# A bidirectional decay scan on VectorE, rewritten as one fp32 matrix product per channel on TensorE

## What is computed

```python
# ek = exp(ctx), v = ctx, ew = exp(w); carries before token t is absorbed
A2 = ew * A + ekt * vt          # and B2 = ew * Bd + ekt, forward and backward in time
cur = jnp.exp(uc + k)
wkv = (Af + Ab + cur * v) / (Bf + Bb + cur)
x = x + tanh(g_xattn) * sigmoid(layernorm(x)) * wkv
# feed-forward, int8 fake quantisation of activations by one maximum over all of them
xq = act_fake_quant(layernorm(x), clip_x)
h = act_fake_quant(silu(xq @ gate.T) * (xq @ up.T), clip_down)
x = x + tanh(g_ffn) * (h @ down.T)
```

## Time and profile before

| | us |
|---|---|
| median of 3 runs | 245.74 (243.35 to 245.87) |
| profiled execution | 245.59 |
| its span | 243.9 |
| attention part, to the first gate product | 153.2 |
| feed-forward part | 90.7 |

### The profile page before, as it was taken

How to read it: one execution, slowest core, us unless ns; L and a number is a source line. 1 busy time by engine, 2 the same in 40 slices (tenths; PEclk the granted TensorE clock), 3 DMA queues, 4 the chain that set the end, 5 groups by cost and what they waited for, 6 DMA issues and landing times.

```text
span 243.9 us, 3531 instructions
## 1 busy us (share of the span) xinstructions
PE 156.2 (64%) x1002; PEld 113.4 (47%) x1002; DVE 219.0 (90%) x307; ACT 166.8 (68%) x220; POOL 121.4 (50%) x151
## 2 busy tenths in 40 slices
PE   0609675476726596556565622999595993689970
PEld 0409565476625485545465612434232341466640
DVE  0999999999999999999999787279999799899993
ACT  5454975929959197393772759799797788689700
POOL 7431444438465384454832740057373575008992
PEclk9955979889999978999987875699998899599995
DMA  5796566610000000000000000000000000002358
GB/s 152 217 336 198 174 203 219 220 50 4 0 0 0 0 0 0 0 0 0 0 0 0 4 0 0 0 1 0 3 0 0 0 0 0 1 3 86 129 180 293
DMA packets 16107, 15.08 MB, mean 62 GB/s; under 512 B 2016, under 2 KB 15840, under 8 KB 16096
## 3 DMA queue, kind: packets, MB, share of 16 engines
q1 hardware_dynamic: 16096, 14.95, 19.2%
HBM read 10.75 MB, written 4.19 MB: 61 GB/s over the span
## 4 chain that ended last, share of the span: by engine, by line
DVE 29%; issue 21%; PE 18%; POOL 14%; ACT 12%; DVEq 2%; DMA 2%; POOLq 1%; SPq 0%; ACTq 0%
DVE hidden L666 9%; PE ps L1012 8%; PE ps L976 7%; DVE hidden L664 3%; POOL rs L357 3%; POOL x_all L334 3%; ACT silu_out L567 2%; POOL hidden L387 2%; POOL hidden L315 2%; DVE h_space L823 2%; DVE h_peaks L789 2%; DMA hidden<-in_ctx 2%; POOL rs L344 2%; DVE hidden L778 2%; DVE x L766 1%
## 5 line engine op out<-in xcount | busy, mean ns | idle before, releaser
L881 PE MATMUL ps<-ident,hidden 128*128 128x128 f32 x128 | 41.4, 323 | 48.5 <-POOL hidden L325 23.7
L881 PEld LDWEIGHTS ps<-ident,hidden 128*128 128x128 f32 x128 | 21.0, 164 | 54.7 <-POOL hidden L325 43.4
L883 PE MATMUL ps<-ident,hidden 128*128 128x128 f32 x128 | 40.2, 314 | 0.0
L885 PE MATMUL ps<-ident,hidden 128*128 128x128 f32 x128 | 40.1, 313 | 0.0
L664 DVE TENSOR_TENSOR_SCAN hidden<-hidden,ps 128x1024 f32<-128x1024 f32 x16 | 36.3, 2269 | 0.0
L666 DVE TENSOR_TENSOR_SCAN hidden<-xq,ps 128x1024 f32<-128x1024 f32 x16 | 36.2, 2262 | 0.0
L443 ACT ACTIVATE hidden<-hidden 128x512 f32<-128x512 f32 x16 | 10.0, 625 | 33.9 <-DVE hidden L677 33.9
L325 POOL TENSOR_TENSOR hidden<-zero_tile 128x18 f32<-128x18 f32 x16 | 3.5, 222 | 56.7 <-DVE hidden L666 56.7
L976 PE MATMUL ps<-xq,wuT 128*128 128x512 bf16 (+1 forms) x96 | 24.8, 402 | 6.4 <-DVE hidden L778 6.2
L1012 PE MATMUL ps<-wdT,z_t 128*128 128x256 bf16 (+1 forms) x192 | 25.4, 288 | 2.6 <-ACT z_t L585 2.6
L789 DVE TENSOR_REDUCE h_peaks<-hidden (+2 forms) x24 | 26.1, 1122 | 0.6 <-POOL hidden L387 0.3
(11 more groups left out here) (91 smaller groups left out, 363.1 us busy)
## 6 DMA issues: line engine op xcount, KB each, us to landing
hidden<-in_ctx SPq DMA_DIRECT2D x8, 512.0 KB, 3.7
x_all<-in_x SPq DMA_DIRECT2D x8, 512.0 KB, 4.6
out<-x_all SPq DMA_DIRECT2D x16, 256.0 KB, 2.2
h_space<-in_L_ffn_w_down SPq DMA_DIRECT2D x1, 704.0 KB, 7.1
z_t<-in_L_ffn_w_gate SPq DMA_DIRECT2D x1, 640.0 KB, 6.2
z_t<-in_L_ffn_w_up SPq DMA_DIRECT2D x1, 640.0 KB, 7.4
z_t<-in_L_ffn_w_gate SPq DMA_DIRECT2D x2, 64.0 KB, 6.4
z_t<-in_L_ffn_w_up SPq DMA_DIRECT2D x2, 64.0 KB, 7.6
```

Source lines behind the costliest of these rows:

```text
L881: nc.tensor.matmul(dst, cur[:, h, q, i * T:(i + 1) * T], ident[:, :], start=True, stop=False, is_transpose=True)
L883: nc.tensor.matmul(dst, scans[:, h, 0, q * UNIT + i * T:q * UNIT + (i + 1) * T], ident[:, :], start=False, stop=False, is_transpose=True)
L885: last = nc.tensor.matmul(dst, scans[:, h, 1, q * UNIT + i * T + 1:q * UNIT + (i + 1) * T + 1], ident[:, :], start=False, stop=True, is_tr ...
```

## The change

The first part is rebuilt. It works on channels, not on groups of sequences:

- `ctx` is loaded whole (8 transfers), and each group is reversed in time by a product with a flipped identity (`reverse`, 2 products of 512 columns a group); ACT takes the exponential from PSUM (8 of 1024 columns), DVE the product `ek * ctx` (8 of 1024 columns).
- ACT makes the 255 lag weights of each channel once and stores them to DRAM (128 x 510 fp32). SP loads, for 8 channels at a time (32 chunks), the 128x128 matrix of each channel as 128 overlapping rows of 128 values: 512 KB a chunk in pieces of 512 B, in 6 slots.
- PE does one fp32 product per channel, 128x128 stationary by 64 moving columns (32 sequences of `ek`, 32 of `pk`, which lie 256 elements apart), into every 8th column of a bank; 6 banks in turn.
- DVE then does per chunk a denominator and a mixed value of 256 columns each, ACT a logarithm and an exponential of 512 columns per pair of chunks, POOL a residual of 512 columns per pair.
- The scans, the transpositions in and out, `cur` and the zeroing are gone.
- All of `x` is loaded, and its first layer norm done for all 8 groups, before the first denominator.
- Second layer norm: the statistics over channels 0 to 127 come from chunk pair 10 on (`early_stats`), those over 128 to 255 after the last residual (`late_stats`). Normalising, transposing, keeping and the maxima of all 8 groups follow after it.
- The three weights are scaled, quantised, cast and turned at fixed places among the chunks.

```diff
-                nc.vector.tensor_tensor_scan(scans[:, h, 0, 1:2 * UNIT + 1], decay[0][:, h, :], src, 0.0,
-                                             ALU.mult, ALU.add)
-                nc.vector.tensor_tensor_scan(scans[:, h, 1, 0:2 * UNIT][:, ::-1], decay[1][:, h, ::-1], src[:, ::-1],
-                                             0.0, ALU.mult, ALU.add).then_inc(s["scan_done"], 1)
...
+            def load_lags(j):
+
+                if j >= SLOTS:
+                    sp.wait_ge(s["ab_done"], j - SLOTS + 1)
+                src = bass.AP(lag_dram, j * CK * LAGS, [[1, P], [LAGS, CK], [1, T]])
+                sp.dma_start(lag_tile[j % SLOTS], src).then_inc(lag_in[j % SLOTS], 16)
...
+            def accumulate(j):
+
+                pe.wait_ge(lag_in[j % SLOTS], 16 * (j // SLOTS + 1))
+                if j == 0:
+                    pe.wait_ge(s["pk_done"], GROUPS)
+                wait(pe, s["mix_done"], j - BANKS + 1)
+                for c in range(CK):
+                    last = nc.tensor.matmul(ps[:, j % BANKS, c:2 * HALF:CK], lag_tile[j % SLOTS][:, c, :],
+                                            ekp[:, j * CK + c:2 * SEQS * C:C], start=True, stop=True)
+                last.then_inc(s["ab_done"], 1)
...
+            for j in range(CHUNKS):
+                accumulate(j)
+                if j == 10:
+                    turn_weights(0)
+                if j == 14:
+                    turn_weights(1)
+                if j == 20:
+                    turn_weights(2)
+            for g in range(GROUPS):
+                turn_z(g)
...
+            for m in range(PAIRS):
+                reciprocal(m)
+                if m == 4:
+                    quantise_weights(0)
+                    cast_weights(0)
+                if m == 6:
+                    keep_weights(0)
+                    quantise_weights(1)
+                    cast_weights(1)
...
+            denominator(0)
+            denominator(1)
+            done = 0
+            for m in range(PAIRS):
+                if m + 1 < PAIRS:
+                    denominator(2 * m + 2)
+                mix(2 * m)
+                if m + 1 < PAIRS:
+                    denominator(2 * m + 3)
+                mix(2 * m + 1)
+                if m == 3:
+                    weight_scales(0)
```

More of the change, by code:

```diff
@@ L99, in gated_rwkv_ffn @@
[L99 to L109, removed]
@@ L203, in gated_rwkv_ffn, with channels @@
         out_v = out.rearrange("b t c -> t b c")
[L205 to L215, removed]
-            for g in range(end, stop or GROUPS + last_skew):
-                step(g)
-        def do_early(early, g, h):
-            for work, m in early.get((g, h), ()) if isinstance(g, int) else ():
-                work(m)
         def seqs(tile, first, n):
-            return tile[:, bass.ds(first * C, n * C)].rearrange("p (b c) -> p b c", c=C)
+            return tile[:, first * C:(first + n) * C].rearrange("p (b c) -> p b c", c=C)
+        def channels(tile, first, n):
+            return tile.rearrange("p (b c) -> p b c", c=C)[:, :, first:first + n]
         @block.sync
@@ L263, in _ @@
[L263 to L269 removed]
+                    sp.wait_ge(s["w_quant"], 1)
+                    sp.dma_start(down[:, :, 0:I], src).then_inc(weights_in[m], 16)
@@ L273, in _ @@
             load_weights(0)
-            next_load(1)
-            load_weights(1)
-            load_weights(2)
-            with sp.Fori(2, GROUPS) as g:
-                next_load(g)
+            for j in range(SLOTS, CHUNKS):
+                load_lags(j)
+                if j == SLOTS + 1:
+                    load_weights(1)
+                if j == CHUNKS // 2:
+                    load_weights(2)
             for n in range(SUMS):
@@ L381, in _ @@
+            for g in range(GROUPS):
+                rstd1(g)
+            for m in range(PAIRS):
+                residual(m)
+            for g in range(GROUPS):
+                rstd2(g)
             with pool.Fori(0, BLOCKS // 2) as pair:
@@ L642, in stats2, with early_stats, late_stats @@
+            def early_stats(first, n):
+                dve.wait_ge(s["x1_done"], PAIRS // 2)
+                for i in range(first, first + n):
+                    stats2(i, 0)
+            def late_stats(g):
+                dve.wait_ge(s["x1_done"], PAIRS)
                 for i in range(GS):
-                    last = nc.vector.bn_stats(bn2[:, i, :], xs[:, i, :])
+                    last = stats2(g * GS + i, 1)
                 last.then_inc(s["bn2_done"], 1)
-                wait(dve, s["bn2_done"], g + 1)
@@ L719, in _ @@
-            iterate(dve, step, 3, 1, GROUPS)
             def sigmoid_clips():
@@ L907, in _, with reverse @@
-            turn_in(0, 0)
+            def reverse(g):
+                pe.wait_ge(ctx_in[g], 16)
+                wait(pe, s["pk_done"], g - 2)
+                for i in range(2):
+                    at_ = g * GC + i * GC // 2
+                    last = nc.tensor.matmul(turned(g)[:, i * GC // 2:(i + 1) * GC // 2], flip[:, :],
+                                            ctx_all[:, at_:at_ + GC // 2], start=True, stop=True)
+                last.then_inc(s["ctx_back"], 1)
+            def accumulate(j):
+                pe.wait_ge(lag_in[j % SLOTS], 16 * (j // SLOTS + 1))
+                if j == 0:
+                    pe.wait_ge(s["pk_done"], GROUPS)
[4 more added lines that the diff above has]
+                last.then_inc(s["ab_done"], 1)
```

589 lines of the change are left out of this document (238 added, 351 removed).

## The result

The changed kernel takes 282.73 us (median of 4 runs, 282.03 to 283.59) beside 244.55 us for the kernel before on the same chip: a ratio of 1.156, with a 95% interval from 1.149 to 1.163. It is slower, as forecast, but by 38 us where 9 were forecast, and it lies outside the range (238 to 280).

A forecast was written before the change was run, and what follows sets the result against it. DVE was taken to bound the attention part, its scans worth 72.5 us. Start to 48.4, loop to 131.2, second norm 31.1 to 162.3, feed-forward 90.7, plus 1.7 gave 254.7 us; range 238 to 280.

The forecast's parts named there:

- 1. `x` landed; first denominator: Start of the attention part: loading `ctx`, `x` and six lag chunks until 42.0, then norm work; first denominator at 48.4 us.
- 2. chunk on PE: Chunk's eight fp32 products: 1.79 us at full clock, twice that at half; each restart loses 2.15 us.
- 3. last residual ends: Chunk loop from 48.4 to 131.2 us, with PE stalling for the three weights' casts; last residual before was at 141.2.
- 4. from there to the first gate product: Second norm of all 8 groups after the last residual, bound by ACT: 31.1 us, where 12 us stood before.
- 5. feed-forward part: Part after the first gate product, claimed unchanged at 90.7 us.
- The third rival: Chunk loop: lag-row transfers set the pace at 3.0 us a chunk, 264 us in total; chance 0.13.
- The rule beside it: Lag loads: pieces off a 256-byte boundary also fetch the bytes before; 2.0 us a chunk, 1.6 by bytes alone.
- The load as the bound: PE's products: two-pass fp32 stationary load sets each pair at 0.112 us, 1.79 a chunk; 64 moving columns need only 53 ns.
- the locks: Chunk loop: weight transpositions queued on PE await ACT's cast, which awaits DVE's scales; three PE stalls of over 6 us.
- The second, strided columns: PE's products: strided read and write each double the stream, 213 ns a pair, 3.4 us a chunk, 289 us; chance 0.12.
- the rule there: PE's products: new 16-byte SBUF lines pay a penalty and non-contiguous PSUM patterns slow matmuls; no factor given.
- The faster rival: Chunk loop: PE not load-bound and keeping its clock, 80 ns a pair, 1.28 us a chunk, 240.4 us; chance 0.30.

The follow-up runs named there:

- everything together: Changed kernel with products of 64 stationary columns, reads and writes side by side, 64 columns streamed once, weights' transpositions later: 226.3 us, 0.925 of the kernel before.
- late turns: Changed kernel with the weights' transpositions on PE behind chunks 13, 20 and 25 instead of 10, 14 and 20, ACT's work moved along: 271.64 us, ratio 1.117.
- the halves: Changed kernel with each product made as two of 64 stationary columns, into the upper and lower 64 partitions, strides kept: 257.05 us (one run).
- the old turns: Kernel with 64-column stationary products and side-by-side reads and writes, weights' transpositions behind chunks 10, 14 and 20 as in the changed kernel: 236.68 us, ratio 0.965.

## Why the prediction was wrong in size and right in sign

| step | forecast | after |
|---|---|---|
| 1. `x` landed; first denominator | 42.0; 48.4 | 42.4; 48.2 |
| 2. chunk on PE | 1.79, 3.6 at half clock | 3.41, always half clock |
| 3. last residual ends | 131.2 | 158.7 |
| 4. from there to the first gate product | 31.1 | 30.3 |
| 5. feed-forward part | 90.7 | 91.6 |

**The start** held to 0.2 us at the first denominator. The lag rows' pieces of 512 B, for which no row stood, ran between those of `ctx` and `x` at a mean of 312 GB/s (the second window of the result), which makes 1.7 us a chunk by bytes; almost alone in a full queue they took 1.8 (everything together, 291 GB/s). I had taken 2.0 and bounded by 3.2. The third rival, lag rows that set the pace, is out: none of PE's waits in the changed kernel was for `lag_w`; what its loop waited for most is the cast:

```profile
PE ps L804 <- ACT w_intb L437: 10.2, 3, 3.7
```

The rule beside it (the Trainium skill, DMA: Bandwidth & Descriptors, How a descriptor splits into AXI transactions) asked for 2.0 us, as an estimate. Both stretches give less than that and more than the 1.6 us that the bytes cost at 329 GB/s, so these runs neither bear the rule out in full nor put it aside.

**The load as the bound** held. A pair took 111 ns in the 2.6 us at full clock with late turns, and 213 at half clock, as forecast from the 59 ns by which the shortest fp32 load of L990 exceeds a transposition's. It took the same with the strides gone (213) and with twice the columns, read without a step (111 and 213), so neither stream nor strides set it, and a pair with half the stationary columns took less. That these figures are a load of two passes fits their length at both clocks; no run takes the load alone.

**The clock was the step that failed.** With the same turns and the clock allowed to rise, the loop ended 3 us from its forecast (128.2 and 128.3 for 131.2), so its other terms were right in sum. Step 2 says: "I give each restart after a stall 4.3 us at half clock: 2.15 us lost." It takes for granted that TensorE, once its products run back to back, is at 2.4 GHz within some microseconds, since both restarts before did so the earlier trace rows. They did it with other work: transpositions of 128 moving columns, which are as many as they load in, and wide bf16 products. The new products stream 64 columns behind a load of 128, so that PE was busy all the time and moved columns in at most half of it. The granted clock stayed at 1.2 GHz from 25.6 to 192.8, through 37.56 us without a gap. With late turns it fell from 2.4 while such products ran. With the same loads and twice the columns it rose. What the clock asks for I can't say from these runs; that "PE busy" in the profile is not enough, they show. The Trainium skill, TensorE: Matmul & The Clock Gate, section What's actually happening, ties the clock to how busy the engine has been; by the profile's busy time this trace does not agree, with PE busy for those 37.56 us and the clock at 1.2 GHz.

The loop's 27.5 us come out of it piece by piece, against the forecast's times for PE being free (70, 86.2, 104.6, then the last residual at 131.2) and the chain's (73.4, 92.2, 117.0, 158.7): 3.4, 2.6, 6.4 and 15.1 us more. The last piece is 11 chunks at 3.41 in place of 1.79 (17.8), less the 1.3 that I had added for the clock and 1.5 that the end took less than my 5.6 (4.1). In the earlier ones the locks hid a part of the slower products, since PE waited less for the weights' casts, 10.2 us in all and at most 3.7 (the row above), where I had "three PE stalls of over 6 us". With the same turns and a read without a step they were 15.0, at most 5.3, and with the halves 17.9, at most 6.2. That part of step 3, the lock itself, stands: moving the turns gave 11 and 10 us back.

**The rivals.** The second, strided columns, named 213 ns a pair and 289 us, and 282.7 is the nearest of all forecasts; a reader of the total alone would take it as the winner. The pair is right and the mechanism is not: without any step the pair was 213 ns too, and 282.6 us. The factor that I let the stream have before it shows, 2.1, turns out to be about what the read's step costs: 0.85 ns a column and pass where the load's passes go at 0.42 at full clock. Hence at 64 columns it hides exactly (111 ns with it), and at 128 it doesn't (219). Of the rule there (the Trainium skill, Advanced Engine Details and Errata, Memory Cachelines), the SBUF half agrees with the runs, with this factor of two; the PSUM half doesn't: every eighth column written cost nothing that these runs show (206 ns a pair averaged, with and without the step, at a strided read; 111 ns either way without one).

The faster rival asked for an engine not bound by its loads at a clock that stays up. The changed kernel had neither, but the version with halves has the first, and it is 7.5% faster. With the old turns it took 236.7, near the rival's 240.4; with the later ones, which the rival didn't have, 226.3.

**The second norm** held: 30.3 for 31.1, ACT busy 24.9 of it. The feed-forward part held within its spread.

A range of 238 to 280 left the case "half clock throughout" out, though it could have been priced from rows of before: 3.6 a chunk stood in my own text as "twice that at half clock". That is 1.8 us more for each of the 21 chunks from 11 on, 38 us in all, less what the locks hide.

## What to carry to other kernels

For a matrix product, set the columns that it streams beside the columns that it loads. Where the load takes longer, TensorE can be busy without a gap and stay at 1.2 GHz, as here for a whole loop, so price such a loop at both clocks; half the stationary columns a product, or twice the moving columns a load, brought the clock back in these runs. A moving operand that is read in steps of 1 KB is worth laying out again where the copy hides under a load, while a wait of one engine for another's weight work can be cured by moving that work to where the queue behind it has slack, 10 and 11 us here. And the largest wait in a page is a candidate, not a cause: without the lag rows on which PE had waited 19.5 us, the loop ended where it had.

## What the runs showed of the hardware that I had not expected

- TensorE ran at 1.2 GHz for 167 us, 25.6 to 192.8, in a kernel that kept it busy 77% of its span, and fell from 2.4 to 1.2 GHz amid back-to-back products (late turns, at 27.6).
- Moving fp32 columns read with a step of 1 KB take 0.85 ns a column and pass whatever the clock (218 to 220 ns a pair at 1.2 GHz and at 2.4): raising the clock gains nothing there.
- Products of 64 stationary columns for the upper and the lower 64 partitions overlap. Without a step their starts alternate, mostly 7 and 52 ns apart at full clock and 7 and 100 at half clock: 58 and 107 ns on average for two half loads where one full load takes 111 and 213, so the halves together cost about half of what they replace.
- The same feed-forward part took from 89.6 to 94.8 us over these kernels, roughly in step with its mean granted clock: 94.6 to 94.8 at 0.84, 91.6 to 92.0 at 0.87, 89.6 to 91.7 at 0.89 or more. Before it was 90.7 at 0.90. A difference of 4 us between single runs is looked for there first.
